# A decoder layer on one core: rows of the second cross group loaded earlier, first rows scaled on VectorE, two value copies, feed-forward rows turned within the last cross group

## The reference

```python
x = x + attn(layernorm(x))          # 32 query heads, 8 key/value heads of 32, binary (sign) weights with scales
x = x + xattn(layernorm(x), ctx)    # 16 heads of 64; low-rank queries (1024 -> 128 -> 1024), low-rank keys/values (1024 -> 64)
x = x + ffn(layernorm(x))           # U1 1024 -> 256, V1 -> 2 x 2752, silu(gate) * up, U2 -> 256, V2 -> 1024, biases
```

## Time and profile before

| | us |
|---|---|
| median of 3 runs | 1520.04 (1519.54 to 1523.94) |
| the profiled execution | 1523.0, its span 1521.2 |
| PE busy | 1383.8 (91%) |
| VectorE, ScalarE, GpSimd busy | 906.7, 707.1, 517.7 |
| self-attention up to the last projection | 0 to 665 |
| cross attention, four groups | 665 to 1034 |
| feed-forward | 1034 to 1521 |

### The profile page before, as it was taken

One profiled execution on the slowest core, in us unless ns is written; L12 is line 12 of the kernel. 1 busy time (PEld: TensorE's weight loads), 2 busy tenths in 40 slices (PEclk: granted clock), 3 DMA queues, 4 the chain that ended last, 5 costly groups with the idle time before them and its releaser, 6 DMA issues.

```text
span 1521.2 us, 22619 instructions
## 1 busy us (share of the span) xinstructions
PE 1383.8 (91%) x8423; PEld 979.3 (64%) x8423; DVE 906.7 (60%) x1611; ACT 707.1 (46%) x1589; POOL 517.7 (34%) x461
## 2 busy tenths in 40 slices
PE   5888899999989998869889898886999999999998
PEld 3555455545555555437667676664888888888886
DVE  5468555845673668447577485572663763763645
ACT  5166602550353145317657375562554354353452
POOL 2037602870576157402121121032442342342330
PEclk9999999999999999999999999997999999999999
DMA  5767644655548364265546353348010310310111
GB/s 194 98 133 133 128 75 113 105 90 108 112 70 130 93 127 106 70 193 141 144 107 171 97 154 102 90 135 308 24 58 0 111 56 1 111 56 1 70 69 56
DMA packets 94881, 157.55 MB, mean 104 GB/s; under 512 B 9910, under 2 KB 49076, under 8 KB 94772
## 3 DMA queue, kind: packets, MB, share of 16 engines
q1 hardware_dynamic: 94772, 156.11, 41.9%
HBM read 82.15 MB, written 25.17 MB: 71 GB/s over the span
## 4 chain that ended last, share of the span: by engine, by line
PE 66%; DMA 10%; DVE 10%; ACT 5%; issue 4%; SPq 3%; POOL 2%; DVEq 0%; POOLq 0%; ACTq 0%
PE bank L982 15%; PE bank L994 7%; PE bank L898 7%; DMA q_stack<-hi_lo 6%; PE bank L774 5%; PE bank L967 3%; PE bank L808 3%; PE bank L728 3%; PE bank L788 3%; PE bank L856 2%; PE bank L821 2%; PE bank L883 2%; PE bank L1007 2%; DMA xq_stack<-xhi_lo 2%; PE bank L868 2%
## 5 line engine op out<-in xcount | busy, mean ns | idle before, releaser
L1529 POOL TENSOR_TENSOR fold<-wide 128x512 f32<-128x512 f32 x128 | 163.5, 1286 | 245.9 <-ACT wide L1062 226.1
L1062 ACT ACTIVATE wide<-bank 128x512 f32<-128x512 f32 x256 | 151.2, 597 | 146.4 <-PE bank L808 144.2
L1588 POOL TENSOR_TENSOR v_lo<-v_all,v_hi 128x512 fp32r<-128x512 f32 x88 | 122.6, 1395 | 246.5 <-ACT v_hi L1169 246.5
L1337 DVE TENSOR_REDUCE neg_top<-bank 128x2 f32<-128x512 f32 x256 | 171.1, 680 | 58.9 <-PE bank L788 57.9
L808 PE MATMUL bank<-q_stack,k_stack 98*128 98x512 f32 x256 | 140.1, 548 | 3.9 <-ACT wide L1062 3.9
L982 PE MATMUL bank<-pT_hi,v_hi 128*128 128x512 f32 x352 | 137.3, 390 | 2.6 <-POOL v_lo L1588 2.6
L982 PE MATMUL bank<-pT_hi,v_lo 128*128 128x512 f32 x352 | 137.2, 390 | 0.0
L982 PE MATMUL bank<-pT_lo,v_hi 128*128 128x512 f32 x352 | 136.9, 389 | 0.0
L1486 DVE SCALAR_TENSOR_TENSOR inner<-bank,b_cols,inner 128x512 f32<-128x512 f32 x88 | 65.9, 749 | 112.7 <-PE bank L982 109.4
L788 PE MATMUL bank<-k_stack,q_stack 96*128 96x256 f32 x512 | 112.4, 307 | 19.7 <-DMA q_stack<-hi_lo 15.8
L788 PEld LDWEIGHTS bank<-k_stack,q_stack 96*128 96x128 f32 x512 | 94.7, 196 | 47.9 <-DMA q_stack<-hi_lo 21.3
(11 more groups left out here) (176 smaller groups left out, 3141.7 us busy)
## 6 DMA issues: line engine op xcount, KB each, us to landing
q_stack<-hi_lo SPq DMA_DIRECT2D x96, 256.0 KB, 5.9
xin<-x_scratch SPq DMA_DIRECT2D x32, 512.0 KB, 4.5
xq_stack<-xhi_lo SPq DMA_DIRECT2D x128, 128.0 KB, 2.4
x_res<-in_x SPq DMA_DIRECT2D x22, 512.0 KB, 5.0
x_scratch<-x_res SPq DMA_DIRECT2D x16, 512.0 KB, 2.8
xin<-in_ctx SPq DMA_DIRECT2D x16, 512.0 KB, 4.7
x_res<-x_scratch SPq DMA_DIRECT2D x16, 512.0 KB, 4.0
x_group<-x_scratch SPq DMA_DIRECT2D x32, 256.0 KB, 3.5
```

The costliest lines, as they stand in the source:

```text
L1062: act.activation(PT[m % PT_RING][:, :], tiles[m % 2][:, :], ACT.Exp).then_inc(sem["tile_exped"], 1)
L1337: dve.tensor_reduce(neg_top[U % 2][:, r, b, :], tops[n % 2][:, :].rearrange("p (a b) -> p a b", a=QT), AX.X, ALU.max, negate=True).then_in ...
L1529: pool.tensor_tensor(fold[f % FOLD_RING][:, :], PT[2 * f % PT_RING][:, :], PT[(2 * f + 1) % PT_RING][:, :], ALU.add).then_inc(sem["folded" ...
L1588: pool.tensor_tensor(lo[:, :, :, 0:n], inner_gu(f, n), hi[:, :, :, 0:n].bitcast(F32), ALU.subtract).then_inc(sem["iw_lo"], 1)
```

## The change

It makes these edits:

- Three loads of group 1's `y` rows move from behind the `xg_load` steps into the output projection of self-attention, and the first `norm` with them, behind part 5.
- The four `y` rows of group 0 are scaled by a new step `apply` on VectorE, three steps after their `norm`; GpSimd keeps the power.
- `attnT_raw` exists twice; `mix_out(U)` waits for `finish(U-2)`. The statistics tiles `bn` are four in the attention stages.
- The four `z` rows of feed-forward group 0 are loaded, normalised, turned and split within the last cross group, and both halves of `u1` are loaded and split there (`u1_split` on GpSimd, `u1_rest` on VectorE). `down` becomes the first PE work of the feed-forward stage, and `b1` comes behind it.
- `u2_all` and `zT` move to the front of the feed-forward tiles in memory, so that `hT3` and `u1s` lie over tiles that are free once the last `lowq` and `lowkv` are done (`rows_low`).

```diff
@@ self_order
             for m, at in enumerate((38, 40, 44, 45)):
                 put(at, ("load", "y", 0, m))
                 put(at + 6, ("norm", "y", 0, m))
+                put(at + 9, ("apply", "y", 0, m))
...
-            order += late[0] + late[1] + [("raw_split", 0), ("o_load", g, 1)] + o_parts(g, 0)[0]
-            order += late[2] + late[3] + late[4] + [("lowq", 0), ("lowq_out", 0), ("raw_split", 2)] + late[5]
+            order += late[0] + late[1] + [("raw_split", 0), ("o_load", g, 1), ("load", "y", 1, 0)] + o_parts(g, 0)[0]
+            order += late[2] + late[3] + late[4] + [("lowq", 0), ("lowq_out", 0), ("raw_split", 2), ("load", "y", 1, 1)] + late[5]
...
                 if i == 2:
-                    order.append(("raw_split", 3))
+                    order += [("raw_split", 3), ("load", "y", 1, 2)]
+                if i == 5:
+                    order.append(("norm", "y", 1, 0))
+def z_turn(g, i):
+    return [("turn", "z", g, i // 2, i % 2), ("split", "z", g, i // 2, i % 2)]
@@ cross_order
-        else:
-            order += [load(1, t) for t in range(3)]
...
-        if g + 1 < NG:
+        if 0 < g < NG - 1:
             lead.insert(0, [("norm", "y", g + 1, 0)])
...
             for j in range(TILES):
-                side.setdefault((3 + j) * XUH, []).append([("load", "z", 0, j)])
+                side.setdefault(j * XUH, []).append([("load", "z", 0, j)])
             for j in range(TILES):
-                side.setdefault((4 + j) * XUH, []).append([("norm", "z", 0, j)])
+                side.setdefault((1 + j) * XUH, []).append([("norm", "z", 0, j)])
+            for i in range(2 * TILES):
+                side.setdefault(10 + 2 * i, []).append(z_turn(0, i))
+            for i, at in enumerate((5, 15)):
+                side.setdefault(at, []).append([("u1_load", i)])
+                side.setdefault(at + 6, []).append([("u1_split", i)])
+                side.setdefault(at + 10, []).append([("u1_rest", i)])
@@ ffn_order
-    order = [("u1_load", 0), ("u2_zero",)]
-    for i in range(2 * TILES):
-        order += turn(0, i)
...
-    order += [("b1",), ("b1_out",)]
+    order = [("u2_zero",), ("iw_load", 0), ("b1_load",), ("iw_load", 1)]
     down = lambda g, i: [("down", g, i // 2, i % 2)] + ([("down_out", g, i // 2)] if i % 2 else [])
     for i in range(2 * RB):
         order += down(0, i)
-    order += [("b2_load",), ("iw", 0, 0), ("iw", 0, 1)]
+        if i == 1:
+            order += [("b2_load",), ("iw", 0, 0)]
+    order += [("iw", 0, 1), ("b1",), ("b1_out",)]
@@ build_program
-    OTs_self = sb("attnT_raw", [P, GT], F32, mem)
+    OTs_self = [sb(f"attnT_raw{i}", [P, GT], F32, mem) for i in range(2)]
+    def normed(step):
+
+        if step[1:] in ON_VECTOR:
+            return sem["y_applied"], step[3] + 1
+        return sem["ln_done"], POOL_NORM[step] + 1
+    def rows_low(e):
+
+        for kind in ("lowq_out", "lowkv_out"):
+            _, full, use = bank_of(kind, NG - 1)
+            e.wait_ge(full, use + 1)
@@ scalar_program, mix_out
-                if U:
-                    e.wait_ge(sem["attn_out"], U)
-                act.activation(OTs_self[:, :], mixed[:, :], ACT.Copy).then_inc(sem["mix_copied"], 1)
+                if U > 1:
+                    e.wait_ge(sem["attn_out"], U - 1)
+                act.activation(OTs_self[U % 2][:, :], mixed[:, :], ACT.Copy).then_inc(sem["mix_copied"], 1)
@@ vector_program
+            elif kind == "apply":
+                k = NORM[("norm", *at)]
+                buf, land, count = row_of("load", *at)
+                st = bn[BN_OF["norm", *at][0]]
+                e.wait_ge(sem["ln_pow"], k + 1)
+                dve.tensor_scalar(buf[:, :], buf[:, :], st[:, 12:13], st[:, 15:16], ALU.add, ALU.mult).then_inc(
+                    sem["y_applied"], 1)
```

More of the change, by code:

```diff
@@ L300, in ffn_order @@
 def ffn_order():
-    turn = lambda g, i: [("turn", "z", g, i // 2, i % 2), ("split", "z", g, i // 2, i % 2)]
-    order = [("u1_load", 0), ("u2_zero",)]
-    for i in range(2 * TILES):
-        order += turn(0, i)
[L305 to L312, removed]
-    order += [("b1",), ("b1_out",)]
+    order = [("u2_zero",), ("iw_load", 0), ("b1_load",), ("iw_load", 1)]
     down = lambda g, i: [("down", g, i // 2, i % 2)] + ([("down_out", g, i // 2)] if i % 2 else [])
@@ L329, in ffn_order @@
             for i in range(2 * TILES):
-                plan[i + 9].append(turn(g + 1, i))
+                plan[i + 9].append(z_turn(g + 1, i))
             for i in range(2 * RB):
@@ L416 @@
 NORM = ordinals("norm")
+BN_OF = {}
+for _step, _k in NORM.items():
+    _b = _k % (2 if _step[1] == "z" else 4)
+    BN_OF[_step] = (_b, next((s for s in reversed(BN_OF) if BN_OF[s][0] == _b), None))
+ON_VECTOR = [("y", 0, m) for m in range(TILES)]
+POOL_NORM = {s: i for i, s in enumerate(s for s in NORM if s[1:] not in ON_VECTOR)}
 SIGN = ordinals("sign")
@@ L466, in build_program @@
     attn_mem = ExitStack()
+    bn += [sb(f"bn{i}", [P, 16], F32, attn_mem) for i in range(2, 4)]
     ident16 = sb("ident16", [P, P], F16, attn_mem)
@@ L524, in build_program @@
     mem = ExitStack()
+    u2_all = sb("u2_all", [P, FB, RANK], F32, mem)
+    zT = [sb(f"zT_{n}", [P, RB, GT], F32R, mem) for n in ("hi", "lo")]
     hT3 = [sb(f"hT3_{n}", [P, KB, GT], F32R, mem) for n in ("hi", "lo")]
@@ L654, in group_turned @@
         e.wait_ge(sem["split_lo"], max(SPLIT["split", ph, g, m, 1] for m in range(TILES)) + 1)
+    def rows_low(e):
+        for kind in ("lowq_out", "lowkv_out"):
+            _, full, use = bank_of(kind, NG - 1)
+            e.wait_ge(full, use + 1)
     def turned_free(e, ph, g):
+        if ph == "z" and g == 0:
+            rows_low(e)
         if ph == "c" and g == 0:
@@ L1450, in vector_program @@
                 t.then_inc(sem["xnormed"], 1)
-            elif kind == "u1_split":
+            elif kind == "u1_rest":
                 i = at[0]
@@ L1533, in gpsimd_program @@
                 buf, land, count = row_of("load", *at)
-                st = bn[k % 2]
+                st = bn[BN_OF["norm", *at][0]]
                 e.wait_ge(sem["ln_stat"], 3 * k + 3)
@@ L1537, in gpsimd_program @@
                 pool.tensor_tensor(st[:, 15:16], st[:, 14:15], neg_half[:, :], ALU.pow).then_inc(sem["ln_pow"], 1)
-                e.wait_ge(sem["ln_pow"], k + 1)
-                pool.tensor_scalar(buf[:, :], buf[:, :], st[:, 12:13], st[:, 15:16], ALU.add, ALU.mult).then_inc(
-                    sem["ln_done"], 1)
+                if tuple(at) not in ON_VECTOR:
+                    e.wait_ge(sem["ln_pow"], k + 1)
+                    pool.tensor_scalar(buf[:, :], buf[:, :], st[:, 12:13], st[:, 15:16], ALU.add, ALU.mult).then_inc(
+                        sem["ln_done"], 1)
             elif kind == "finish":
```

14 lines of the change are left out of this document (6 added, 8 removed).

## The result

On one chip, in turn with the kernel before, the changed kernel took 1505.0 us in the median of four runs (1503.5 to 1508.6), the kernel before 1521.0 (1519.5 to 1523.9). The ratio is 0.9884, with an interval of 0.9858 to 0.9911: faster by 18 us (the medians differ by 16). The forecast was 1491, with a range that ended at 1502. The direction was right, 1505 lies outside. Run twice more on other chips, the changed kernel gave ratios of 0.9886 (0.9868 to 0.9904) and 0.9880 (0.9860 to 0.9900). One of the four executions of loads_only, a kernel further down, took 2722 us and is left out of its ratio.

What follows compares the result with a forecast made beforehand. TensorE, busy 91% of the span, was taken as the bound, with time to win where it idles or runs slow. 10.5 + 5.0 + 19.8 - 6.5 = 28.8 us off 1523.0 gave 1494.2, median 1491, range 1484 to 1502.

Steps and rivals of the forecast that it cites:

- the sum of all worst bounds: Whole kernel: all parts at their worst bounds together give 1504 us, called unlikely.
- D: Last cross group: added z turns and u1 work lengthen it, costing 6.5 us, bounds 3 and 10.
- The last line of the sum: Whole kernel: profiled 1523.0 less 28.8 gives 1494.2 us; the median of runs lies 3.0 lower, 1491.
- B: Start of cross attention's second group: earlier y loads remove PE's 9.24 us wait and slow clock, gaining 10.5, bounds 8 to 11.5.
- A: End of self-attention: apply on VectorE and two attnT_raw copies shorten PE's waits, gaining 5.0 us, bounds 1 and 8.
- The rule that spoke against the part: Applies on VectorE: two-port-mode instructions contend with GpSimd for SBUF, so folds beside them would lengthen; no size given.
- C: Cross attention to feed-forward: down starts at once, gate/up at 1042.3 instead of 1062.1, gaining 19.8 us, bounds 17 and 21.
- A pair becomes ... 9.4: Last cross group: a pair of heads takes 8.0 - 0.7 + 0.75 + 1.35 = 9.4 us, four pairs cost 5.6.
- rival (6): Last cross group becomes a chain through two banks, 4.4 us for each of eight turns; at 6, time 1532; chance 0.03.
- The 0.9 us booked: Last cross group: two u1 subtractions on VectorE and two more 512 KB loads ahead of xq_stack add 0.9 us.
- The sign that I had named: Last cross group: the forecast is wrong if this group grows by over 10 us.

Runs made afterwards that it cites:

- loads_only: Kernel before with only the three y loads of group 1 and the first statistics moved beside the output projection; ratio to the kernel before 0.9930.
- ab_only: Changed kernel with z rows and u1 loaded and turned where they were before, memory order as before; ratio to the kernel before 0.9910.
- turns_apart: Changed kernel with z turns at steps 8+4m and 11+4m of the last cross group, not every even step from 10; ratio to the kernel before 0.9812.
- rest_late: Changed kernel with only VectorE's two u1_rest subtractions moved from side steps 15 and 25 to 26 and 29; ratio to the kernel before 0.9858.
- four_bn: Kernel before with four bn tiles in place of two, all else as it was; ratio to the kernel before 1.0002.
- two_bn_again: Second run of the changed kernel with two bn tiles instead of four; ratio to the kernel before 0.9858.
- after_third: Changed kernel run once more unchanged, beside two-tile kernels on the same chip; ratio to the kernel before 0.9880.
- after_again: Unchanged copy of the changed kernel, run again for a second profile; ratio to the kernel before 0.9886.

## Why the forecast was right, and where it was wrong

The direction and the places of the gains were right; the time came out 14 us above the forecast and above even the sum of all worst bounds, 1504. Two steps of the sum failed: D's term took the wait for one bank and left out the other, and the longer transfers from shifted tiles had no term at all. The last line of the sum, from the traced execution to the median, failed too.

**B, right.** Forecast -10.5 with no wait at the first turn and clock 1.00; the stretch shows -10.5 and the ratio -10.7. The wait of 9.2 is gone and PE is busy for 1.7 us less; next late is an exponential, 0.35 us. That it fits to a tenth is luck: two traces of the kernel before differ by 1.5 us in this stretch.

**A, right in size, partly by luck.** Forecast -5.0; ab_only's stretch is 16.4 shorter, less B that is 5.9. The second copy is worth 7.5: 3.8 of waiting where I had 4.2, and 3.6 by the clock where I had 1.5. The applies were booked at 0.7 and cost 1.5; the two errors have opposite signs. One apply's price was set at 1.1 us, of bounds 0.35 and 1.41; in the trace they took 0.79 and 1.04 us, and 1.75 and 1.68, two of them above the upper bound. The estimate of 0.7 us worked out from the Trainium skill (VectorE: DVE Perf Modes, the perf-mode tier table) is near the shortest, 0.79. The rule that spoke against the part holds as well, as the last section shows.

**C, right.** Forecast -19.8, measured -19.2, -17.9 and -19.3. The weights landed at 1040.6 (forecast 1040.3), gate/up came 14.2 us after the last `xfin`. These times can be compared because that `xfin` stands at 1028.5 in the one trace and at 1028.8 in the other.

**D, the step that failed first.** Forecast -6.5, measured -9.4, -10.3 and -10.2. The term "A pair becomes ... 9.4" took one bank's wait, 1.35 us before `xfin`, and the runs show 1.2 each: right. It left out the other bank, 3.6 us in all. The sequence turn, `xq`, turn, `xfin` gives the second turn the bank of the first, and its evacuation stands in VectorE's queue behind statistics. Pairs took 10.1 to 11.8 us, not 9.4. It is close to the mechanism of rival (6), which I priced at 4.4 us a turn and gave 0.03; at the 0.4 to 2.2 us that it took, it belonged into the sum. turns_apart shows it: there D is 1.9 us above the kernel before. The 0.9 us booked for the `u1` subtractions and late `xq_stack` loads came from the former alone: rest_late takes 1.1 us off the wait for the low part, and the waits for `xq_stack` shrank, 5.6 to 2.3. The sign that I had named, a last group longer by over 10 us, showed in two of three traces.

**The address shift, the term that was missing.** The change adds two `bn` tiles of 64 bytes a partition ahead of attention's tiles, and the sum has no term for it. It costs about 4.7 us by the start stretches, of which 3.2 are waiting of PE, and 3.8 to 6.7 by the pairs of ratios. I read the `bn` edit as bookkeeping. That it slows the 2 KB packets and makes PE wait longer is shown. How much of the median it costs is less sure: two pairs show it, while four_bn's median (+0.3, interval -1.7 to +2.4) shows none, though its trace has 56.8 us of idle PE in the start stretch where the kernel before has 54.3 and 54.2. Why its median doesn't show these 2.5 us is open.

**The bookkeeping.** 28.8 us forecast; less 3.5 for D, 1.0 for C, 4.7 for the shift, plus 0.5 in A and B, leaves 20.1. The three traces show 19.5 to 22.3, the ratios 17.4 to 18.3 (of 1521 to 1524). The 2 to 3 us between traces and ratios are within what single executions scatter. From trace to trace the change gained 19.5 of the 28.8, which is 9.3 of the 14 us missed. The other 4.5 lie in the step from trace to median: I took 3.0 off, from 1523.0 to the median of three runs, 1520.0, while the changed kernel's traced execution was the fastest of four, its median 1.5 above it. Over the other chips the kernel before had medians of 1522.2 to 1524.1.

## What to carry to other kernels

When a step is put between others that share banks, write down for each bank who fills it and who empties it, and what stands ahead of the emptying on its engine: here moving eight transposes by one or two steps gave back 8 us of 10. Put a new small tile behind the large ones that DMAs read and write, or take its shift as a change of its own; compare the queue's time for the same bytes before and after. Here a second copy of a tile that passes through three engines was worth more than moving work off the engine that reads it last.

## What the hardware showed that I hadn't expected

**Packets and addresses.** 128 bytes of shift made 2 KB packets 4.5% longer (190.0 to 191.5, then 198.3 to 200.5 ns). The Trainium skill (DMA: Bandwidth & Descriptors, How a descriptor splits into AXI transactions) says that when a descriptor doesn't start at a multiple of 256 bytes, its first transaction starts at the boundary below, and the unused bytes before its own start still cost beats of 32 bytes on the bus. The longer packets go in that direction, but the traces don't show the tiles' absolute addresses, and no run tried another shift: that alignment is the cause is not shown.

**VectorE and GpSimd.** Timelines of VectorE and of GpSimd in the changed kernel:

```profile
604.73 1.04 DVE L1297 TENSOR_SCALAR xin<-xin,bn 128x1024 f32<-128x1024 f32 x1
...
606.48 0.79 DVE L1297 TENSOR_SCALAR xin<-xin,bn 128x1024 f32<-128x1024 f32 x1
...
612.19 1.75 DVE L1297 TENSOR_SCALAR xin<-xin,bn 128x1024 f32<-128x1024 f32 x1 [1.54 <-POOL bn L1566]
...
614.47 1.68 DVE L1297 TENSOR_SCALAR x_res<-x_res,bn 128x1024 f32<-128x1024 f32 x1
...
606.47 1.97 POOL L1577 TENSOR_TENSOR attnT<-attnT_raw,recip_rows 128x512 f32<-128x512 f32 x1 [1.25 <-DVE recip_rows L1388]
...
612.11 1.29 POOL L1558 TENSOR_TENSOR fold<-wide 128x512 f32<-128x512 f32 x1
```

At 606.48 the apply takes 0.79 us, and GpSimd's `attnT` beside it 1.97 in place of its usual 1.28, 0.69 more. At 612.19 a fold that began 0.08 us earlier takes its usual 1.29, and the apply 1.75, 0.96 more than the shortest. One of the two waits for nearly all of the other's instruction. two_bn_again and after_third show the same four durations within 0.02 us. The Trainium skill (SBUF — State Buffer, SBUF: two separate sides) describes the shared ports as a lock held for a whole instruction; the trace agrees.

**Clock and time.** Runs of one kernel differ with their mean granted clock: after_again had 1500.7 us at 0.987 and 1511.1 at 0.981, the kernel before 1521.4 at 0.979 and 1526.7 at 0.974. What makes the clock differ from run to run is not shown.
